# Second expert product two tiles later, two routing banks, first weights by SyncE, second image's normalisation on ScalarE

## What is computed

```python
x = x + _L0_conv_ref(_ln_c(x), ...)     # 4 dilated 3x3 branches, projection, group norm, relu
t = _to_tokens(x)
t = t + _L0_ffn_ref(_ln_t(t), ...)      # 8 experts, top 2 of a softmax router
x = _from_tokens(t, x)

# _moe: for each expert e
    h = jax.nn.gelu(tokens @ w1[e] + b1[e], approximate=False)
    y = h @ w2[e] + b2[e]
    out = out + combine[:, e:e + 1] * y
```

## Time and profile before

| | before |
|---|---|
| median of 3 runs | 2249.96 us (2245.78 to 2255.39) |
| profiled execution | 2248.74 us |
| its span | 2246.9 us |
| mean granted TensorE clock | 0.923 |
| TensorE, matmuls | 1910.4 us busy, 85% |
| VectorE | 1560.9 us, 69% |
| ScalarE | 1333.7 us, 59% |
| POOL | 1083.1 us, 48% |
| DMA | 459.87 MB, mean 205 GB/s |

### The profile page before, as it was taken

The page is one execution under the profiler, slowest core; times in us unless marked ns, Lnnn a source line. Parts: engine busy times, 40 slices in busy tenths (PEclk is TensorE's granted clock), DMA queues, the critical chain, the costliest instruction groups (busy, mean ns, idle before and its releaser), DMA issues.

```text
span 2246.9 us, 56560 instructions
## 1 busy us (share of the span) xinstructions
PE 1910.4 (85%) x20204; PEld 1832.1 (82%) x20204; DVE 1560.9 (69%) x4184; ACT 1333.7 (59%) x2877; POOL 1083.1 (48%) x1430
## 2 busy tenths in 40 slices
PE   5899799999969997999998895888888868999943
PEld 4899798999859997898888884888887768999932
DVE  4577675666556775777777774688887856777765
ACT  4677343333327774556556541887777758888822
POOL 3666212222215663145655562367777775555510
PEclk9999799999979998999999997898899989999965
DMA  4332597567554434677888879567667667888889
GB/s 143 105 106 78 145 294 189 141 173 174 153 142 133 132 102 111 190 228 216 227 232 245 237 209 322 171 219 227 224 218 225 202 192 274 284 282 283 280 310 368
DMA packets 341802, 459.87 MB, mean 205 GB/s; under 512 B 82677, under 2 KB 262709, under 8 KB 339173
## 3 DMA queue, kind: packets, MB, share of 16 engines
q1 hardware_dynamic: 231208, 246.52, 38.7%
q10 hardware_dynamic: 68433, 109.55, 14.9%
q0 software_dynamic: 41888, 100.18, 13.0%
HBM read 291.86 MB, written 174.69 MB: 208 GB/s over the span
## 4 chain that ended last, share of the span: by engine, by line
PE 46%; ACT 14%; DVE 13%; POOL 9%; issue 7%; DMA 7%; ACTq 3%; SPq 1%; POOLq 1%; DVEq 1%
PE ps_y L424 17%; PE ps_a L424 7%; PE ps_o L1050 6%; PE ps_b L987 4%; POOL expert_in L2148 4%; PE ps L424 3%; ACT w_now L1494 3%; POOL expert_out L2224 3%; ACT e_act L1483 3%; DMA o_acc<-res_scratch 3%; PE ps_tok L897 1%; DVE cat_lo L1938 1%; PE ps_o L1037 1%; ACT h_hi L1486 1%; DMA y_scratch<-y_acc 1%
## 5 line engine op out<-in xcount | busy, mean ns | idle before, releaser
L424 PE MATMUL ps_y<-cat_hi,wp 128*128 128x288 f32 x2048 | 483.5, 312 | 1.8 <-DVE cat_lo L1938 1.8
L2224 POOL DMA_INDIRECT expert_out<-e_out,e_dest x320 | 327.4, 1023 | 248.2 <-DVE e_out L2048 177.2
L2202 POOL DMA_DIRECT2D patches<-rows_scratch x340 | 190.4, 604 | 499.3 <-PE ps_o L1037 301.4
L424 PEld LDWEIGHTS ps_y<-cat_hi,wp 128*128 128x128 f32 x2048 | 354.4, 195 | 2.0 <-DVE cat_lo L1938 2.0
L2148 POOL DMA_INDIRECT expert_in<-r_ln,r_pos x288 | 290.0, 1007 | 106.3 <-issue 86.3
L2168 POOL TENSOR_TENSOR taps<-taps,g_rows 96x108 f32<-96x108 f32 (+2 forms) x416 | 243.8, 611 | 162.5 <-ACT g_rows L1310 158.6
L1379 ACT ACTIVATE bands<-ps_b 112x288 f16<-112x288 f32 (+4 forms) x256 | 105.1, 411 | 345.4 <-PE ps_b L987 331.9
L424 PE MATMUL ps_y<-cat_lo,wp 128*128 128x288 f32 x1024 | 308.1, 301 | 0.0
L424 PE MATMUL ps<-w,h_hi 128*128 x1280 | 258.5, 301 | 53.9 <-DVE h_lo L2037 51.1
L1938 DVE SCALAR_TENSOR_TENSOR cat_lo<-ps_o,cat_hi 128x288 fp32r<-128x288 f32 (+1 forms) x576 | 228.2, 419 | 92.9 <-ACT cat_hi L1385 89.4
L424 PE MATMUL ps<-e_hi,w_now 128*128 128x256 f32 x1280 | 266.1, 292 | 4.8 <-ACT w_now L1494 2.1
(11 more groups left out here) (201 smaller groups left out, 4488.3 us busy)
## 6 DMA issues: line engine op xcount, KB each, us to landing
e_x<-expert_in SPq DMA_DIRECT2D x160, 260.0 KB
patches<-rows_scratch SPq DMA_DIRECT2D x160, 192.0 KB
patches<-rows_scratch SPq DMA_DIRECT2D x256, 108.0 KB
patches<-rows_scratch SPq DMA_DIRECT2D x204, 112.0 KB
x_in<-in_x SPq DMA_DIRECT2D x48, 384.0 KB, 3.7
rows_scratch<-rows_st SPq DMA_DIRECT2D x48, 384.0 KB, 4.2
r_x<-in_x ACTq DMA_DIRECT2D x72, 256.0 KB
r_y<-y_scratch ACTq DMA_DIRECT2D x72, 256.0 KB
```

What stands on the lines that cost most here:

```text
L424: mm = eng.matmul(out, lhs[p], rhs[q], start=start and n == 0, stop=stop and n == 2)
L2202: pool.dma_start(patch_target(s, n), patch_source(m, s, n)).then_inc(patch_pooled[s % RING], 16)
L2224: pool.indirect_dma_start(out=ys_dram, out_offset=bass.IndirectOffsetOnAxis(ap=e_dest[:, i, j:j + 1], axis=0), in_=e_out[:, u, j], in_offs ...
```

## The change

It has these parts:

1. `second_product` and `output` of a tile come two iterations later instead of one (BEHIND = 2), with three buffers of `h_hi` and `h_lo` instead of two (HB = 3). `hidden(n)` gets a wait for `h_lo_done` of tile n - 1.
2. The second image's routing uses two PSUM banks `ps_r` in turn; `r_raw` is copied in two halves per pair, one from each bank (before: one copy).
3. In the first half SyncE loads each tile's `w1_now` directly from device memory (`load_first_weights`, 512 KB each), one tile ahead of need and behind the load of the next tile. The copies `weights_hi` of tiles 0 to 79 and ScalarE's two early loads of `w1` are gone; the whole `w1` (4096 KB) is loaded by SyncE at tile 24, for the second half, where `weights_hi` stays.
4. The second image's `norm_tile` moves from VectorE to ScalarE (an ACTIVATE with Identity, scale and bias), one tick later, behind a wait for VectorE's `r_resd`.
5. EARLY is 4 instead of 5. The scatters of POOL come behind `send(placed // 4 - 2 + q)` instead of `- 1 + q`.

```diff
-EARLY = 5
-EARLY_W = 3
+EARLY = 4
+BEHIND = 2
+HB = 3
+W1_AT = 24
...
-        h_hi = sbuf(ctx, "h_hi", [128, 2, CC, S], F32R)
-        h_lo = sbuf(ctx, "h_lo", [128, 2, CC, S], F32R)
+        h_hi = sbuf(ctx, "h_hi", [128, HB, CC, S], F32R)
+        h_lo = sbuf(ctx, "h_lo", [128, HB, CC, S], F32R)
...
+                ps_r = psum(r2, "ps_r", [128, 2, 512])
+            with ExitStack() as r2:
+                psum(r2, "first_routing", [128, 512])
...
+            def load_first_weights(n):
+
+                u = n % 2
+                e = sp.value_load(etable[0][0:1, 0, n:n + 1], min_val=0, max_val=E - 1)
+                after(sp, e_first, n - 1)
+                sp.dma_start(w1_now[:, u:u + 1].rearrange("p u z c f -> p u (z c f)").bitcast(F32),
+                             w_dram[0, :, ds(e, 1)].rearrange("p u z c -> p u (z c)")).then_inc(w_now_loaded[u], 16)
+
             sp.wait_ge(out_ready, UNITS + unit(62))
             for n in range(EX):
                 load_tile(n)
+            sp.wait_ge(out_ready, 2 * UNITS)
+            for n in range(2):
+                load_first_weights(n)
             kept = 2 * CPAIRS
             for n in range(EX, STREAM):
                 load_tile(n)
+                if 2 <= n - 1 < ETILES:
+                    load_first_weights(n - 1)
+                if n == W1_AT:
+                    sp.wait_ge(proj_done, 4 * IMAGES * STEPS)
+                    sp.dma_start(w1[:].rearrange("p e z c -> p (e z c)").bitcast(F32),
+                                 w_dram[0].rearrange("p e z c -> p (e z c)")).then_inc(w_loaded_1, 16)
...
+                bank, raw = (ps_k, t % TP) if t < ITILES else (ps_r[:, t % 2], t % TP // 2)
...
-                    after(pe, r_kept, slots_before(r, k))
+                    after(pe, r_kept, slots_before(r, max(k - 1, 0) if r else k))
...
-                pe.wait_ge(w_hi_ready, n + 1)
+                if n < ETILES:
+                    pe.wait_ge(w_now_loaded[u], 16 * (n // 2 + 1))
+                else:
+                    pe.wait_ge(w_hi_ready, n - ETILES + 1)
...
-                if n == 1:
+                if n == BEHIND:
                     pe.wait_ge(w_loaded_2, 16)
-                if n:
-                    second_product(n - 1)
+                if n >= BEHIND:
+                    second_product(n - BEHIND)
                 routing(1, 4 * n + 2)
                 routing(1, 4 * n + 3)
-            second_product(STREAM - 1)
+            for n in range(STREAM - BEHIND, STREAM):
+                second_product(n)
...
+                    bank = ps_r[:, k % 2] if r else ps_k
+                    last = act.activation(r_ln[:, p % HELD, k % TP, 0:C], bank[:, 0:C], ACT.Copy)
+                    if r and k % TP >= TP - 2:
+                        after(act, r_read, p - 1)
+                        odd = r_raw[:, p % 2].rearrange("p (k b e) -> p k b e", b=2, e=E)[:, :, k % 2]
+                        last = act.activation(odd, bank[:, 256:256 + TP // 2 * E].rearrange("p (k e) -> p k e", e=E), ACT.Copy)
+                    elif not r and k % TP == TP - 1:
...
+                if p >= CPAIRS:
+                    act.wait_ge(r_resd, TP * p + i + 1)
                 act.activation(r_ln[:, p % HELD, i, 0:C], r_ln[:, p % HELD, i, 0:C], ACT.Identity,
                                bias=r_nmr[:, p % 2, i:i + 1], scale=r_rstd[:, p % 2, i:i + 1]).then_inc(r_lnd, 1)
...
-                    p = plan.pair_end.get(u - 7 - 2 * i)
-                    if p is not None and not r:
+                    p = plan.pair_end.get(u - 7 - r - 2 * i)
+                    if p is not None:
...
-            act.dma_start(w1[:, 0:EARLY_W].rearrange("p e z c -> p (e z c)").bitcast(F32),
-                          w_dram[0, :, 0:EARLY_W].rearrange("p e z c -> p (e z c)")).then_inc(w_loaded_1, 16)
             act.wait_ge(proj_done, 4 * IMAGES * STEPS)
-            act.dma_start(w1[:, EARLY_W:E].rearrange("p e z c -> p (e z c)").bitcast(F32),
-                          w_dram[0, :, EARLY_W:E].rearrange("p e z c -> p (e z c)")).then_inc(w_loaded_1, 16)
             act.dma_start(w2[:].rearrange("p e z c -> p (e z c)").bitcast(F32), w_dram[1].rearrange("p e z c -> p (e z c)")).then_inc(w_loaded_2, 16)
...
+                after(act, h_lo_done, n - 1)
...
-            act.wait_ge(w_loaded_1, 32)
-            weights_hi(0)
-            weights_hi(1)
...
+                    act.wait_ge(w_loaded_1, 16)
+                if ETILES <= n + 2 < STREAM:
...
-                if n:
-                    output(n - 1)
+                if n >= BEHIND:
+                    output(n - BEHIND)
...
-                return plans[1].placed(p) // 4 - 1 + q
+                return plans[1].placed(p) // 4 - BEHIND + q
```

More of the change, by code:

```diff
@@ L323, in build @@
         res_early = sbuf(ctx, "res_early", [128, EARLY, TT, C])
-        sbuf(ctx, "to_wp", [128, 1280], mybir.dt.uint8)
+        sbuf(ctx, "to_wp", [128, 256], mybir.dt.uint8)
         w2 = sbuf(ctx, "w2", [128, E, 2, CC * C], F32R)
@@ L348, in build @@
             with ExitStack() as r2:
-                psum(r2, "routing", [128, 512])
+                ps_r = psum(r2, "ps_r", [128, 2, 512])
+            with ExitStack() as r2:
+                psum(r2, "first_routing", [128, 512])
                 ps_g = psum(r2, "ps_g", [128, 2, 256])
@@ L852, in rank_pair @@
             def rank_pair(p):
-                out = ps_k[:, 304:304 + (TP + 1) * E]
+                out = (ps_k if p < CPAIRS else ps_r[:, 0])[:, 304:304 + (TP + 1) * E]
                 pe.wait_ge(r_eith, p + 1)
@@ L1136, in second_product @@
                     for f in range(CC):
-                        mm = three_passes(pe, ps_2[:, u, j], [z[:, u, f, j * 128:(j + 1) * 128] for z in (h_hi, h_lo)],
+                        mm = three_passes(pe, ps_2[:, u, j], [z[:, n % HB, f, j * 128:(j + 1) * 128] for z in (h_hi, h_lo)],
                                           [w2[:, ds(e, 1), p, f * C:(f + 1) * C].rearrange("p o f -> p (o f)")
@@ L1230, in keep_slot @@
                         act.wait_ge(r_scattered[p % HELD], 16 * TP * TOP * (p // HELD))
-                    last = act.activation(r_ln[:, p % HELD, k % TP, 0:C], ps_k[:, 0:C], ACT.Copy)
-                    if k % TP == TP - 1:
+                    bank = ps_r[:, k % 2] if r else ps_k
[5 more added lines that the diff above has]
+                    elif not r and k % TP == TP - 1:
                         after(act, r_read, p - 1)
@@ L1239, in keep_slot @@
                     after(act, r_based, q)
-                    last = act.activation(r_count[:], ps_k[:, 304:304 + (TP + 1) * E], ACT.Copy)
+                    counted = ps_r[:, 0] if r else ps_k
+                    last = act.activation(r_count[:], counted[:, 304:304 + (TP + 1) * E], ACT.Copy)
                 if k < ITILES or ranked is not None:
@@ L1727, in residual @@
                                   ALU.mult, ALU.add).then_inc(r_resd, 1)
-            def norm_tile(p, i):
-                dve.tensor_scalar(r_ln[:, p % HELD, i, 0:C], r_ln[:, p % HELD, i, 0:C], r_rstd[:, p % 2, i:i + 1],
-                                  r_nmr[:, p % 2, i:i + 1], ALU.mult, ALU.add).then_inc(r_lnd, 1)
             done = [0]
@@ L1821, in routing @@
                         residual(r * CPAIRS + p, i)
-                    p = plan.pair_end.get(u - 7 - 2 * i)
-                    if p is not None and r:
-                        norm_tile(r * CPAIRS + p, i)
                 for part in range(3):
@@ L2036, in hidden_lo @@
                 dve.wait_ge(h_hi_done, n + 1)
-                dve.tensor_tensor(h_lo[:, u], e_act[:, u], h_hi[:, u].bitcast(F32), ALU.subtract).then_inc(h_lo_done, 1)
+                dve.tensor_tensor(h_lo[:, n % HB], e_act[:, u], h_hi[:, n % HB].bitcast(F32), ALU.subtract).then_inc(h_lo_done, 1)
             def output(n):
@@ L2125, in _ @@
                     weigh_second(g)
-            output(STREAM - 1)
+            for n in range(STREAM - BEHIND, STREAM):
+                output(n)
             for g in range(GROUPS_OUT, 2 * GROUPS_OUT):
```

8 lines of the change are left out of this document (4 added, 4 removed).

## The result

| | before | after |
|---|---|---|
| median | 2249.74 us of 4 runs | 2272.93 us of 4 runs (2269.27 to 2276.75) |
| profiled execution, span | 2246.9 us | 2267.5 us |
| mean granted clock | 0.923 | 0.926 |

A forecast was written before the change was run, and what follows sets the result against it. POOL's 266 indirect DMAs were taken to pace the middle, with the gain coming before it. Terms -6 - 5 - 2 + 1.5 + 2 + 2 - 2 + 2 = -7.5 us gave median 2242 us, range 2226 to 2263.

The forecast's parts named there:

- Start: 1377 to 1407 us, DMA engines full: w1 loads leave, two w_now loads enter; -6 us, ends -9 and 0.
- nothing at the start: Rival: w_now stands last in SyncE's queue in the same jam, so -6 becomes 0; 2248 to 2250 us; chance 0.12.
- Early tiles: 1412 to 1477 us: ScalarE drops a copy per tile, TensorE need not wait for h_lo; -5 us, ends -9 and 0.
- Middle: 1477 to 1833 us, paced by POOL's 266 DMAs: savings elsewhere cost at nothing, -2 us, lower end -10.
- The 1.2 us per tile: From tile 13 on, compute was taken to run ahead of POOL by this much, a lead of 13 us at tile 24.
- DMA: In the middle, 256 of 270 us demanded, share 0.95; later landings +1.5 us, ends 0 and +20 (DMA-bound rival, 0.18).
- upper end of 0 to +10: Whole w1 load at tile 24 delays later SyncE loads; landing at 15 us stalls compute 6; +2 us taken.
- faster rival: The middle shrinks too: fewer collisions on POOL (-8), early tiles at their lower end (-9); -22, 2228 us; chance 0.20.
- Boundary: Between the halves: w_now of tile 79 asked for later, one second product more for TensorE; +2 us, ends 0 and +6.
- Second half: Tiles from 1846 to 2140 us: ScalarE's work unchanged, it waits less for TensorE until 1885; -2 us, ends -6 and 0.
- Output: Output stage: one residual group less loaded early, a deeper queue drains at the end; +2 us, ends 0 and +4.
- The signs: Listed for the profile after: right included POOL gapless for 350 to 357 us; wrong included w_now waits over some 10 us.

## Why the prediction was wrong, point by point

**Start: right in kind, too small in this profile.** Forecast -6 between -9 and 0; measured -10.4. The other profiles with the weights' part spread: the first Gelu came at 1409.93, 1401.82 and 1406.17, with the weights as before at 1411.73. So the start is 2 to 10 us earlier with the part; the rival "nothing at the start" describes one profile of the four (-1.9) better than the forecast does.

**Early tiles: forecast -5, measured -2.6.** The granted clock did rise from 0.92 to 1.00, and the share of the DMA engines from 0.56 to 0.90; with the weights as before, the first expert_in came at 1479.42, no earlier than before. From the first Gelu on that stretch then took 67.7 us, as before (67.8). So the gain there comes with the weights, not with the second product's place, as far as one profile each can tell.

**Middle: the step that failed.** It reads "All this I cost at nothing, since POOL issues the same 266 DMAs." POOL does issue them, at durations no longer than before (means of 999 and 1024 ns, 1019 and 1037 in the earlier trace rows). But the sentence stands on the tiles staying ahead of POOL, and I argued that only from the work that ScalarE loses (35 us net), not from what it waits for. Nor was the lead measured. The 1.2 us per tile that add up to 13 us at tile 24 are in no trace: e_out of the tiles 20 to 24 was ready 7.0, 1.8, 0.3, 1.0 and 0.3 us before POOL sent it in the kernel before, 1.8, 0.6, 0.3, 0.3 and 3.7 with the normalisation on VectorE, and 0.3, 0.6, 2.0, 1.7 and 4.5 in the changed kernel. The new wait for r_resd was seen, and priced at 0.61 us of work each. I did not ask what VectorE does in that tick: it may be in the row of operations that picks the experts of a pair, 5.9 us long with what is interleaved in the case shown above, and ScalarE's e_hi, and with it the next tile's first product, stands behind the wait. Measured: 53 us of waiting by ScalarE, 32.5 us at POOL, +21.8 where I had -2 + 1.5 + 2 for the middle and its loads; with the normalisation back, 353.1 us and thus +1.0. Of the 53 us only a part reached POOL, and how much by the wait and how much by the work stays open.

**DMA: the demand was right, the reader was not.** The share was forecast at 0.95 and came out at 0.91. I looked for the harm at the first product's wait for w_now; that was 0.8 us. The late ones were r_y on ScalarE's queue (1.9 us of waits become 45) and e_x (11.5 us). The load of w1 landed after 18.8 us, near the 15 that I took; the loss of 10.9 us between tiles 20 and 24 was just above the upper end of 0 to +10. In the kernel with the normalisation on VectorE the same four tiles lost 4.9 us, of which 3.2 showed at POOL. That upper end of +10 took all that is issued after w1 on its queue to wait for the whole of it; no run shows such an order. What was seen: in the changed kernel an e_x issued at 1509.38, 5.1 us behind w1 on SyncE's queue, was turned only at 1524.52, and w1 had landed at about 1504.3 + 18.8 = 1523.1. But an r_y issued at 1505.49 on ScalarE's queue, which has no w1, was used only at 1528.66, after 11.7 us of waiting. So the place behind w1 on one queue isn't what all the late loads share.

**POOL's own durations.** The prediction has it that the moved normalisation is not what stretches POOL, and its faster rival took 8 us off for fewer collisions. The mean expert_in takes 999 and 999 ns in the two profiles of the changed kernel and 1002 without the weights' part, against 1019 before and 1021 and 1017 where the normalisation is VectorE's. So these DMAs are shorter where the normalisation is off VectorE, by about 0.02 us x 144 = 2.9 us; expert_out shows no such difference (1024, 1019, 1040 against 1038, 1019, 1010). Why they are shorter isn't shown. They couldn't decide the outcome beside the 32.5 us that POOL waited.

**Boundary: +2, measured +1.1** up to tile 80. The second product that is one more was booked here, but falls due behind the last tile: +3.0 there. From h_hi of tile 159 to the last expert_out it is 6.3 us in the kernel before and with the weights' part alone, and 9.0 to 9.3 in the four profiles with the later second product.

**Second half: -2, measured +4.8**, and this is not explained. It was +4.5 in the second profile of the changed kernel and 7.6 with the weights as before, but -0.1 with the normalisation on VectorE and 0.0 with the weights' part alone, though no normalisation runs in this half. In the three slower ones there are single stops of 2 to 4 us (a late e_x, ScalarE at its own DMA issues), and near them stretches of 10 us in which the granted clock falls from 1.00 to 0.83 (1890 to 1900 and 1960 to 1970 us in the changed kernel). But with the weights' part alone it is 0.83 from 1880 to 1890 us too, and nothing is lost. Why the stops come there and not in the others stays open.

**Output: +2, measured +2.9.**

**The signs.** Of those named as right, the first Gelu (near 1405; 1401.5), the first expert_in (near 1468; 1466.7) and the vanished waits for h_lo in the second half came. POOL without a gap did not, nor did VectorE wait longer than 14.6 us for expert_out DMAs: it waited 10.4. Of those named as wrong, the gaps on POOL came and the waits for w_now did not, so the signs pointed at the middle but at the wrong cause.

## What to carry to other kernels

When a stage is paced by one engine, a change on the others is free only as long as their lead over it lasts, so measure that lead first: when each tile is ready, and when the pacing engine turns to it. Here it was 3.4 us in the median. A moved operation and its wait can use it up even where an engine has less work in sum (here ScalarE, with 233 us in the middle instead of 271). Price a moved instruction by what it waits for and by what is queued behind it on its new engine, in the tick where the engine that it waits for is at its longest chain; a place behind the operations that the next tile needs, or some ticks later, is what this suggests, but no run here showed that it helps. Added DMA traffic is in the same position: the weights' part cost the middle 3 us by itself and 11.7 us beside the normalisation.

## What the runs showed that was not expected

A DMA share of 0.90 to 0.93 over 350 us lets the loads of 0.5 MB with one tile of lead land in time (0.3 to 1.8 us of waits for w_now in four kernels), while ScalarE's loads of 256 KB, issued about one block ahead, come late for 31 to 54 us in sum.
